# A graph layer on one core: one of four transposed chunks made by a block-wise load and VectorE, the sums turned elsewhere

## The chip, the core and the metric

The kernel runs on one core of a Trainium2 chip. The metric is the device time of one execution in microseconds. The kernel before took 223.35 us (median of 3 runs, 223.28 to 223.63).

## The reference

For each of 16 graphs there is a node matrix `x` (512 x 128) and an adjacency matrix `adj` (512 x 512), both float32. The layer normalises `x`, applies relu, and takes the maximum over seven relations.

```python
h = maximum(layernorm(x), 0)
A = [adj, adj, shifted, adj.T, adj.T, shifted.T, eye]          # by relation r = 0..6
HW = einsum('bnf,rfo->rbno', h, W[:, :F]) + einsum('rd,rdo->ro', W_edges, W[:, F:])[:, None, None, :]
AHW = einsum('rbnm,rbmo->rbno', A, HW)
out = x + AHW.max(axis=0) + b
```

As the reference calls it, both adjacency arguments are `adj`. `shifted` is the identity rolled by one row. The constant of each relation is multiplied by the row sums of `adj` (relations 0 and 1) or its column sums (3 and 4).

## The kernel before, in words

A batch is one graph. The order of the work is written out by hand for each engine, with semaphores between engines; there is no scheduler. Buffers that end in 0 and 1 are used by even and odd batches. Step `b` finishes the products of batch `b`, the relations of batch `b-1`, and prepares batch `b+1` ("ahead"). Steps 0 and 1 are unrolled, steps 2 to 13 are a loop of two steps, steps 14 and 15 are unrolled, and a tail follows.

Every float32 operand of a matrix product is split into a rounded part `_hi` and a remainder `_lo`, and each product is three matmuls (`passes`, lines 764 to 767: hi x hi, lo x hi, hi x lo). In one step TensorE does:

- `fwd` of chunks 0 to 3 (bank `fwd_ps`, from the transposed adjacency `at_hi`, `at_lo`) and `bwd` of chunks 0 to 3 (bank `bwd_ps`, from `a_hi`, `a_lo`), 24 matmuls;
- `eye` for three relations and `along` for four (of the batch before), 21 matmuls into the banks `rel_ps`;
- `turn_a` (line 734): for each column chunk `i` of `adj`, four 128x128 transposes against the identity into bank `at_ps[i % 2]`, for the batch ahead; chunks 0 and 1 after `along` of relation 1, chunks 2 and 3 at the end of the step;
- `turn_h` (four transposes of the activations) and `turn_sums` (one, of the 8 columns of sums, into `rel_ps[1]`; line 756).

ScalarE rounds each `adj` chunk to `a_hi` (`round_a`, line 384) and each transposed chunk to `at_hi` (`round_at`, line 389), and sums the rows as it does so; it also normalises, fills a relation's bank with sum times constant (`fill`, line 431), copies the turned sums to SBUF (`take_sums`, line 426) and writes the first relation to `best` (`join_first`). VectorE makes the remainders `at_lo` (`split_at`, line 562), `fwd_lo`, `bwd_lo` and `ht_lo`, takes the maxima (`join`) and turns the result (`turn_best`, which exchanges within 32x32 blocks). So that this is enough, the result is stored, and `x` and `bias` are loaded, by `load_by_blocks` and `store_by_blocks` (lines 201 to 208): four DMAs of 512 pieces of 128 bytes, which put each 32x32 block where its exchange needs it. GpSimd makes `a_lo` and `h_lo`, the inverse deviation, and the last additions.

SyncE starts the DMAs, in order: in a step it reloads `x` and the four chunks of `adj` for batch `b+2` (each waits for `a_lo` of its chunk), stores batch `b-2`, writes the sums to memory and reads them back broadcast over all partitions (`spread_sums`), and loads the blocks of `x`.

## Time and profile before

| | us |
|---|---|
| median of 3 runs | 223.35 |
| the profiled execution's own time | 223.7 |
| its span in the profile | 221.7 |
| TensorE busy | 211.5 (95%) |
| ScalarE busy | 186.0 (84%) |
| VectorE busy | 179.2 (81%) |
| GpSimd busy | 163.8 (74%) |
| DMA, share of 16 engines (the main queue) | 70.3% |

PE is TensorE, PEld its weight loads, DVE is VectorE, ACT ScalarE, POOL GpSimd, SPq the queue of SyncE. An engine's busy time counts overlapping instructions once. Matmuls are pipelined, so the time one costs is the distance from its start to the next start, and not its own length. The name of a line in the profile (L745) is a line of the kernel before; line numbers of the changed kernel are higher (`passes` is at lines 813 to 815, `turn_a` at 792, `turn_sums` at 810).

### The profile page before, as it was taken

How to read it: one execution, taken by the hardware profiler on the slowest of the kernel's cores; microseconds unless marked ns; L12 is line 12 of the kernel's file. 1: busy time of each engine (PE TensorE's matmuls, PEld its weight loads, DVE VectorE, ACT ScalarE, POOL GpSimd, SP SyncE). 2: the span in 40 equal slices, each digit the busy share in tenths (PEclk: the TensorE clock that was granted, in tenths of full speed). 3: DMA queues.
4: the chain of work that ended last, by engine and by line, in shares of the span. 5: the costliest groups of instructions: out<-in, count | busy, mean ns of one | idle time of the engine just before them, and what ended most of it. 6: DMA issues, size and time to landing. Idle time of an engine off the chain costs nothing.

```text
span 221.7 us, 4960 instructions
## 1 busy us (share of the span) xinstructions
PE 211.5 (95%) x1069; PEld 174.5 (79%) x1069; DVE 179.2 (81%) x388; ACT 186.0 (84%) x468; POOL 163.8 (74%) x179
## 2 busy tenths in 40 slices
PE   7898999999999999999999999999999999999980
PEld 5777678887888888888888888888888888887760
DVE  3795799796989879797887969887887969777683
ACT  3767999998998989898898989899898989887640
POOL 1370499979596996969697896969699696969241
PEclk9999999999999999999999999999999999999997
DMA  5928976959596986768596877758597776236725
GB/s 178 302 91 184 243 199 171 263 113 252 135 248 143 245 180 157 231 158 215 122 254 145 198 206 155 235 136 218 131 230 190 165 222 146 43 53 143 158 37 89
DMA packets 91152, 38.71 MB, mean 175 GB/s; under 512 B 71575, under 2 KB 80903, under 8 KB 91143
## 3 DMA queue, kind: packets, MB, share of 16 engines
q1 hardware_dynamic: 90055, 38.48, 70.3%
q10 hardware_dynamic: 1088, 0.13, 0.4%
q8 instruction: 3, 0.05, 0.1%
q14 instruction: 6, 0.05, 0.1%
HBM read 34.33 MB, written 4.26 MB: 174 GB/s over the span
## 4 chain that ended last, share of the span: by engine, by line
PE 85%; DVE 6%; ACT 2%; DMA 2%; issue 2%; SPq 0%; DVEq 0%; ACTq 0%
PE at_ps L745 11%; PE rel_ps L765 11%; PE rel_ps L767 11%; PE rel_ps L766 11%; PE bwd_ps L765 6%; PE bwd_ps L767 6%; PE bwd_ps L766 6%; PE fwd_ps L765 6%; PE fwd_ps L767 6%; PE fwd_ps L766 6%; PE turn_ps L753 3%; DMA a_sb<-in_adj 2%; DVE h_lo L692 1%; DVE best L595 1%; PE rel_ps L762 1%
## 5 line engine op out<-in xcount | busy, mean ns | idle before, releaser
L304 POOL TENSOR_TENSOR a_lo<-a_sb,a_hi 128x512 fp32r<-128x512 f32 x62 | 79.1, 1298 | 37.8 <-ACT a_hi L386 37.8
L595 DVE TENSOR_TENSOR best<-rel_ps,best 128x512 f32<-128x512 f32 x62 | 42.6, 687 | 13.7 <-PE rel_ps L767 13.6
L566 DVE TENSOR_TENSOR at_lo<-at_ps,at_hi 128x512 fp32r<-128x512 f32 x62 | 41.2, 685 | 8.2 <-ACT at_hi L394 7.6
L434 ACT ACTIVATE rel_ps<-sum_all,c_col 128x512 f32<-128x512 f32 (+1 forms) x63 | 41.8, 679 | 4.5 <-DVE best L595 2.9
L386 ACT ACTIVATE a_hi<-a_sb 128x512 fp32r<-128x512 f32 x64 | 39.4, 617 | 3.8 <-DMA a_sb<-in_adj 3.8
L394 ACT ACTIVATE at_hi<-at_ps 128x512 fp32r<-128x512 f32 x62 | 36.3, 590 | 6.5 <-PE at_ps L745 6.3
L745 PEld LDWEIGHTS at_ps<-ident,a_sb 128*128 128x128 f32 x240 | 28.1, 141 | 4.2
L745 PE MATMUL at_ps<-ident,a_sb 128*128 128x128 f32 x240 | 31.2, 272 | 0.0
L592 DVE SCALAR_TENSOR_TENSOR best<-rel_ps,c_col,best 128x512 f32<-128x512 f32 x32 | 23.9, 747 | 6.9 <-PE rel_ps L767 5.8
L319 POOL TENSOR_TENSOR xb_sb<-xp_sb,bias_sb 128x512 f32<-128x512 f32 x16 | 22.7, 1421 | 5.9 <-DMA xp_sb<-in_x 5.9
L765 PE MATMUL bwd_ps<-a_hi,h_hi 128*128 128x512 f32 x64 | 27.0, 421 | 0.0
L765 PE MATMUL fwd_ps<-at_hi,h_hi 128*128 128x512 f32 x64 | 26.6, 416 | 0.4 <-DVE at_lo L566 0.4
L767 PE MATMUL bwd_ps<-a_hi,h_lo 128*128 128x512 f32 x64 | 25.4, 397 | 0.0
L766 PE MATMUL bwd_ps<-a_lo,h_hi 128*128 128x512 f32 x64 | 25.3, 395 | 0.0
L767 PE MATMUL fwd_ps<-at_hi,h_lo 128*128 128x512 f32 x64 | 25.2, 394 | 0.0
L766 PE MATMUL fwd_ps<-at_lo,h_hi 128*128 128x512 f32 x64 | 25.1, 392 | 0.0
L404 ACT ACTIVATE h_sb<-x_sb,shift,rstd 128x128 f32<-128x128 f32 x60 | 24.6, 482 | 0.0
L765 PE MATMUL rel_ps<-ht_hi,w_hi 128*128 128x512 f32 x48 | 19.3, 403 | 1.4 <-issue 0.9
L326 POOL TENSOR_TENSOR o_sb<-turned,xb_sb 128x512 f32<-128x512 f32 x15 | 19.4, 1293 | 0.0
L767 PE MATMUL rel_ps<-ht_hi,w_lo 128*128 128x512 f32 x48 | 19.0, 396 | 0.0
L766 PE MATMUL rel_ps<-ht_lo,w_hi 128*128 128x512 f32 x48 | 19.0, 396 | 0.0
L312 POOL TENSOR_TENSOR h_lo<-h_sb,h_hi 128x512 fp32r<-128x512 f32 x14 | 18.1, 1294 | 0.4 <-DVE h_hi L560 0.4
(103 smaller groups left out, 438.9 us busy)
## 6 DMA issues: line engine op xcount, KB each, us to landing
a_sb<-in_adj SPq DMA_DIRECT2D x64, 256.0 KB, 3.3
sum_all<-sums_dram SPq DMA_DIRECT2D x16, 512.0 KB, 4.1
x_sb<-in_x SPq DMA_DIRECT2D x16, 256.0 KB, 3.7
xp_sb<-in_x SPq DMA_DIRECT2D x64, 64.0 KB, 3.6
out<-o_sb SPq DMA_DIRECT2D x60, 64.0 KB, 2.0
w_sb<-in_L_gnn_W SPq DMA_DIRECT2D x1, 448.0 KB, 6.0
sums_dram<-sum_rows SPq DMA_DIRECT2D x16, 4.0 KB
bias_sb<-in_L_gnn_b SPq DMA_DIRECT2D x4, 64.0 KB, 2.2
```

The costliest lines, as they stand in the source:

```text
L304: pool.tensor_tensor(a_lo[q][:, j, :], a_sb[q][:, j, :], a_hi[q][:, j, :].bitcast(fp32), ALU.subtract).then_inc(a_lo_ready[j], 1)
L386: act.activation(a_hi[q][:, j, :], a_sb[q][:, j, :], ACT.Copy, accum_out=sums[q][:, 0, j:j + 1]).then_inc(a_hi_ready[j], 1)
L394: act.activation(at_hi[q][:, i, :], at_bank(b, i)[:], ACT.Copy, accum_out=sums[q][:, 1, i:i + 1]).then_inc(at_hi_ready[i], 1)
L404: last = act.activation(h_sb[q][:, j, :], x_sb[q][:, j, :], ACT.Relu, bias=shift[q][:, j:j + 1], scale=rstd[q][:, j:j + 1])
L434: act.activation(to[:, cols], sum_all[q][:, 0 if r in FWD else 1, cols], ACT.Copy, scale=c_col[:, r:r + 1]).then_inc(after_it, 1)
L566: dve.tensor_tensor(at_lo[q][:, i, :], at_bank(b, i)[:], at_hi[q][:, i, :].bitcast(fp32), ALU.subtract).then_inc(at_lo_ready[i], 1)
L592: dve.scalar_tensor_tensor(out=best[q][:], in0=held[:], scalar=c_col[:, r:r + 1], in1=best[q][:], op0=ALU.add, op1=ALU.max).then_inc(joine ...
L595: dve.tensor_tensor(best[q][:], held[:], best[q][:], ALU.max).then_inc(joined[r], 1)
L745: last = pe.transpose(at_bank(b, i)[:, j * P:(j + 1) * P], a_sb[q][:, j, i * P:(i + 1) * P], ident[:])
L765: pe.matmul(out, w_hi_, m_hi, start=start, stop=False, skip_group_check=onto)
L766: pe.matmul(out, w_hi_, m_lo, start=False, stop=False, skip_group_check=onto)
L767: return pe.matmul(out, w_lo_, m_hi, start=False, stop=stop, skip_group_check=onto)
```

## The change

The last column chunk of `adj` is no longer transposed by TensorE (except for batch 0). SyncE loads `adj[b, :, 384:512]` once more by blocks, with the same four DMAs of 512 pieces of 128 bytes, into `a_blocks`; VectorE turns `a_blocks` into `at_last` in SBUF; `round_at` and `split_at` of chunk 3 read `at_last` in place of a PSUM bank. `a_blocks` and `at_last` are single buffers.

The sums are turned into `at_ps[0]` after `fwd` of chunk 1 (batches 2 to 15; for batch 15 that place is the one of before), and ScalarE takes them behind `join_first`. SyncE's step is reordered: `x` first, then the store of the sums, `adj` (as two DMAs of two chunks each), the broadcast, the output, the blocks of `x`, the new blocks. The first step is reordered on TensorE, ScalarE and VectorE.

In the diff "..." marks lines left out.

```diff
@@ -70,6 +71,8 @@
 a_lo = pair(sb, "a_lo", [P, C, N], fp32r)
+a_blocks = sb("a_blocks", [P, N])
+at_last = sb("at_last", [P, N])
 at_hi = pair(sb, "at_hi", [P, C, N], fp32r)
@@ -107,7 +110,14 @@
-def at_bank(b, i):
+def is_batch(b, n):
+
+    return isinstance(b, int) and b == n
+
+def at_from(b, i):
+
+    if i == C - 1 and not is_batch(b, 0):
+        return at_last
@@ -222,19 +230,30 @@
         b = 2 * k + q
-        sp.wait_ge(a_turned[C - 1], b + 1)
-        for j in range(C):
-            sp.wait_ge(a_lo_ready[j], b + 1)
-            load_a(k + 1, q, j)
+        sp.wait_ge(a_turned[C - 2], b + 1)
+        if is_batch(b, 0):
+            sp.wait_ge(first_turned, 1)
+        for first in range(0, C, 2):
+            sp.wait_ge(a_lo_ready[first], b + 1)
+            sp.wait_ge(a_lo_ready[first + 1], b + 1)
+            sp.dma_start(a_sb[q][:, first:first + 2, :],
+                         adj[2 * k + 2 + q, first * P:(first + 2) * P, :].rearrange("(j p) m -> p j m", p=P)
+                         ).then_inc(a_loaded[q][first + 1], 16)
+
+    def load_a_blocks(k, q):
+
+        b = 2 * k + q
+        wait(sp, a_turned[C - 1], b - 1)
+        load_by_blocks(a_blocks, adj[b, :, (C - 1) * P:], a_blocks_loaded)
+
+    def store_sums(k, q):
+
+        sp.wait_ge(sum_rows_ready, 2 * k + q + 1)
+        sp.dma_start(sums_dram[q][:, :], sum_rows[q][:]).then_inc(sums_stored[q], 16)
...
-        b = 2 * k + q
-
-        sp.wait_ge(sum_rows_ready, b + 1)
-        sp.dma_start(sums_dram[q][:, :], sum_rows[q][:]).then_inc(sums_stored[q], 16)
-        if is_batch(b, 0):
-            load_by_blocks(bias_sb, bias, bias_loaded)
+
@@ -246,17 +265,24 @@
-        sums_first = is_batch(2 * k + q, 0) or is_batch(2 * k + q, B - 1)
-        if sums_first:
-            spread_sums(k, q)
-        if more:
+        if more and not is_batch(2 * k + q, 0):
+            reload_x(k, q)
+        if is_batch(2 * k + q, 1):
+            reload_a(k, q)
+        store_sums(k, q)
+        if is_batch(2 * k + q, 0):
+            load_by_blocks(bias_sb, bias, bias_loaded)
+        elif more and not is_batch(2 * k + q, 1):
+            reload_a(k, q)
+        spread_sums(k, q)
+        if is_batch(2 * k + q, 0):
             reload_x(k, q)
...
             store(k - 1, q)
-        if not sums_first:
-            spread_sums(k, q)
         load_xp(k, q)
+        if more:
+            load_a_blocks(k + 1, q)
@@ -267,6 +293,7 @@
         load_a(0, 1, j)
+    load_a_blocks(0, 1)
     sp.dma_start(we_sb[:], W[:, F:FE, :]).then_inc(we_loaded, 16)
@@ -380,7 +407,8 @@
         b = 2 * k + q
-        act.wait_ge(a_loaded[q][j], 16 * (k + 1))
+
+        act.wait_ge(a_loaded[q][j if isinstance(k, int) and k == 0 else j // 2 * 2 + 1], 16 * (k + 1))
         wait(act, bwd_done, b - 1)
@@ -388,10 +416,13 @@
         b = 2 * k + q
-        act.wait_ge(a_turned[i], b + 1)
+        if is_batch(b, 0) and i == C - 1:
+            act.wait_ge(first_turned, 1)
+        else:
+            act.wait_ge(a_turned[i], b if i == C - 1 else b + 1)
         wait(act, fwd_done, b - 1)
         wait(act, sums_turned, b - 1)
-        act.activation(at_hi[q][:, i, :], at_bank(b, i)[:], ACT.Copy,
+        act.activation(at_hi[q][:, i, :], at_from(b, i)[:], ACT.Copy,
                        accum_out=sums[q][:, 1, i:i + 1]).then_inc(at_hi_ready[i], 1)
@@ -446,16 +477,16 @@
         act.activation(w_hi[:], w_sb[:], ACT.Copy).then_inc(w_hi_ready, 1)
-        take_sums(0, 0)
+        take_sums(0, 0, rel_ps[1])
         round_at(*ahead, 0)
...
         normalise(*ahead)
+        round_fwd(0, 0)
         act.wait_ge(c_ready, 1)
         join_first(0, 0)
-        round_fwd(0, 0)
-        round_ht(*ahead)
         round_at(*ahead, 2)
         round_at(*ahead, 3)
+        round_ht(*ahead)
         round_a(*ahead, 0)
@@ -466,9 +497,9 @@
             round_at(k, q, 3)
-        if not left:
-            take_sums(k, q, at_ps[0])
         join_first(k, q)
+        if not second:
+            take_sums(k, q)
         if second:
@@ -488,7 +519,8 @@
             round_at(*ahead, 0)
-            take_sums(k, q)
+            if second:
+                take_sums(k, q, rel_ps[1])
         else:
@@ -552,6 +584,14 @@
+    def turn_a_blocks(k, q):
+
+        b = 2 * k + q
+        dve.wait_ge(a_blocks_loaded, G * 16 * b)
+        if not is_batch(b, 1):
+            dve.wait_ge(at_lo_ready[C - 1], b)
+        dve.transpose(at_last[:], a_blocks[:]).then_inc(a_turned[C - 1], 1)
+
@@ -610,18 +650,19 @@
                           ALU.mult).then_inc(wedge_cols_ready, 1)
+        turn_a_blocks(*ahead)
         split_at(*ahead, 0)
...
         dve.wait_ge(c_multiplied, 1)
-        dve.tensor_copy(c_col[:], rel_ps[0][:, 0:R]).then_inc(c_ready, 1)
+        dve.tensor_copy(c_col[:], turn_ps[:, 0:R]).then_inc(c_ready, 1)
         round_h(*ahead)
+        split_fwd(0, 0)
         dve.wait_ge(h_hi_ready, 2)
...
                           ALU.subtract).then_inc(h_lo_ready, 1)
-        split_fwd(0, 0)
-        split_ht(*ahead)
         split_at(*ahead, 2)
         join(0, 0, EYE[1])
+        split_ht(*ahead)
         join(0, 0, EYE[2])
@@ -640,6 +681,7 @@
             round_h(*ahead)
+            turn_a_blocks(*ahead)
         join(*prev, FWD[1])
@@ -734,15 +776,20 @@
         if i == 0:
-            for j in range(C):
+            for j in range(C) if isinstance(k, int) and k == 0 else (1, 3):
                 pe.wait_ge(a_loaded[q][j], 16 * (k + 1))
-        if i >= 2:
-            pe.wait_ge(at_lo_ready[i - 2], b + 1)
+        if i == 2:
+            pe.wait_ge(at_lo_ready[0], b + 1)
+        elif i == 0:
+            pe.wait_ge(at_lo_ready[2], b)
+            if not is_batch(b, 2):
+                pe.wait_ge(sum_rows_ready, b)
         else:
-            pe.wait_ge(at_lo_ready[i + 2], b)
+
+            pe.wait_ge(at_lo_ready[C - 1 if is_batch(b, 1) else 1], b)
         for j in range(C):
-            last = pe.transpose(at_bank(b, i)[:, j * P:(j + 1) * P], a_sb[q][:, j, i * P:(i + 1) * P], ident[:])
+            last = pe.transpose(at_from(b, i)[:, j * P:(j + 1) * P], a_sb[q][:, j, i * P:(i + 1) * P], ident[:])
         last.then_inc(a_turned[i], 1)
@@ -753,12 +800,13 @@
-    def turn_sums(k, q, to=rel_ps[SUMS_BANK]):
+    def turn_sums(k, q, to=at_ps[0]):
         b = 2 * k + q
...
         pe.wait_ge(at_hi_ready[C - 1], b + 1)
-        if is_batch(b, 0):
-            pe.wait_ge(at_lo_ready[1], 1)
+
+        if not is_batch(b, 1):
+            pe.wait_ge(at_lo_ready[1 if is_batch(b, 0) else 2], b + 1)
         pe.transpose(to[0:S, 0:P], sums[q][:].rearrange("p t c -> p (t c)"), ident[:]).then_inc(sums_turned, 1)
@@ -809,8 +857,10 @@
         else:
-            pe.wait_ge(sum_rows_ready, b + 1)
-            if not (isinstance(b, int) and b == 0):
+
+            if is_batch(b, 0) or is_batch(b, 1):
+                pe.wait_ge(sum_rows_ready, b + 1)
+            if not is_batch(b, 0):
                 pe.wait_ge(joined[EYE[1]], b + 1)
@@ -838,24 +888,24 @@
         bwd(0, 0, 3)
-        turn_sums(0, 0)
+        turn_sums(0, 0, rel_ps[1])
         turn_a(*ahead, 0)
+        turn_a(*ahead, 1)
         fwd(0, 0, 1)
         fwd(0, 0, 2)
-        turn_a(*ahead, 1)
-        fwd(0, 0, 3)
         pe.wait_ge(we_loaded, 16)
         pe.wait_ge(wedge_cols_ready, 1)
-        pe.matmul(rel_ps[0][:, 0:R], we_sb[:], wedge_cols[:], start=True, stop=True).then_inc(c_multiplied, 1)
+        pe.wait_ge(ht_lo_ready, 1)
+        pe.matmul(turn_ps[:, 0:R], we_sb[:], wedge_cols[:], start=True, stop=True).then_inc(c_multiplied, 1)
+        fwd(0, 0, 3)
         pe.wait_ge(w_hi_ready, 1)
         pe.wait_ge(w_lo_ready, 2)
+        eye(0, 0, EYE[0])
+        turn_a(*ahead, 2)
         pe.wait_ge(c_ready, 1)
-        eye(0, 0, EYE[0])
+        turn_h(*ahead)
         eye(0, 0, EYE[1])
-        turn_h(*ahead)
         eye(0, 0, EYE[2])
-        turn_a(*ahead, 2)
-        turn_a(*ahead, 3)
@@ -863,9 +913,8 @@
         fwd(k, q, 1)
-        if not left:
-            pe.wait_ge(at_lo_ready[2], B)
-            turn_sums(k, q, at_ps[0])
+        if not is_batch(b, 1):
+            turn_sums(k, q)
         eye(k, q, EYE[1])
@@ -875,8 +924,9 @@
             turn_h(*ahead)
+        if is_batch(b, 1):
             pe.wait_ge(joined[EYE[1]], b + 1)
-            turn_sums(k, q)
+            turn_sums(k, q, rel_ps[1])
         bwd(k, q, 0)
@@ -886,7 +936,6 @@
             turn_a(*ahead, 2)
-            turn_a(*ahead, 3)
```

TensorE, end of a step and beginning of the next (steps of the loop). `bwd_ps` is the last `bwd`, `fwd_ps` the first `fwd` of the next batch. Before:

```order
L767 MATMUL bwd_ps<-a_hi,h_lo 128x512
L745 MATMUL at_ps<-ident,a_sb 128x128 x8
L765 MATMUL fwd_ps<-at_hi,h_hi 128x512
L766 MATMUL fwd_ps<-at_lo,h_hi 128x512
L767 MATMUL fwd_ps<-at_hi,h_lo 128x512
```

In the change, as far as the turn of the sums:

```order
L815 MATMUL bwd_ps<-a_hi,h_lo 128x512
L792 MATMUL at_ps<-ident,a_sb 128x128 x4
...
L813 MATMUL fwd_ps<-at_hi,h_hi 128x512
L814 MATMUL fwd_ps<-at_lo,h_hi 128x512
L815 MATMUL fwd_ps<-at_hi,h_lo 128x512
L810 MATMUL at_ps<-ident,sums 8x128
L813 MATMUL rel_ps<-ht_hi,w_hi 128x512
```

Four of the eight transposes at the step's end are gone, and the turn of the sums stands between the `fwd` of chunk 1 and the `eye` of relation 5.

VectorE, the middle and the end of a step in the change (`a_blocks` and `at_last` are the new buffers, `best` the running maximum):

```order
L600 CAST h_hi<-h_sb 128x512
L590 REGISTER_ALU
L593 STREAM_TRANSPOSE at_last<-a_blocks 128x512
L635 TENSOR_TENSOR best<-rel_ps,best 128x512
...
L642 STREAM_TRANSPOSE turned<-best 128x512
L606 TENSOR_TENSOR at_lo<-at_ps,at_hi 128x512
L606 TENSOR_TENSOR at_lo<-at_last,at_hi 128x512
L623 TENSOR_TENSOR bwd_lo<-bwd_ps,bwd_hi 128x512
```

The first transpose is new, and the remainder of the last chunk has both of its inputs in SBUF; before, the two remainders were one row, `at_lo<-at_ps,at_hi 128x512 x2`.

ScalarE, around the first relation. Before, and then in the change:

```order
L394 ACTIVATE at_hi,sums<-at_ps 128x512 [waits sums_turned,fwd_done,a_turned3]
L442 ACTIVATE best<-rel_ps,c_col 128x512 [waits best_turned,rel_done2]
L434 ACTIVATE rel_ps<-sum_all,c_col 128x512 [waits sums_spread0,joined3]
```

```order
L425 ACTIVATE at_hi,sums<-at_last 128x512 [waits sums_turned,fwd_done,a_turned3]
L473 ACTIVATE best<-rel_ps,c_col 128x512 [waits best_turned,rel_done2]
L460 ACTIVATE sum_rows<-at_ps 8x128 [waits sums_stored1,sums_turned]
L465 ACTIVATE rel_ps<-sum_all,c_col 128x512 [waits sums_spread0,joined3]
```

The copy of the sums has come between the first relation and the first fill.

## Rows read from the trace of the kernel before

**Rows 1.** The page: busy time of the engines, and the chain that ended last.
```profile
PE 211.5 (95%) x1069; PEld 174.5 (79%) x1069; DVE 179.2 (81%) x388; ACT 186.0 (84%) x468; POOL 163.8 (74%) x179
...
PE 85%; DVE 6%; ACT 2%; DMA 2%; issue 2%; SPq 0%; DVEq 0%; ACTq 0%
```

**Rows 2.** Windows: length, busy of PE, PEld, DVE, ACT, POOL, clock, DMA, GB/s.
```profile
12.00:24.00 12.00, 10.74 (x59) 8.64 (x58) 8.99 (x20) 8.69 (x23) 3.12 (x7) 1.00 0.61 152
48.92:112.44 63.52, 63.52 (x332) 53.00 (x331) 54.05 (x116) 57.16 (x146) 52.28 (x56) 1.00 0.77 194
```

**Rows 3.** Timeline of TensorE, one step: start, length, instruction.
```profile
118.08 1.03 PE L745 MATMUL at_ps<-ident,a_sb 128*128 128x128 f32 x8
118.95 0.60 PE L753 MATMUL turn_ps<-ident,h_sb 128*128 128x128 f32 x4
119.39 0.27 PE L762 MATMUL rel_ps<-ident,sums 128*8 128x128 f32 x1
119.41 0.48 PE L765 MATMUL bwd_ps<-a_hi,h_hi 128*128 128x512 f32 x1
119.73 0.40 PE L766 MATMUL bwd_ps<-a_lo,h_hi 128*128 128x512 f32 x1
119.96 0.39 PE L767 MATMUL bwd_ps<-a_hi,h_lo 128*128 128x512 f32 x1
```

**Rows 4.** Timeline of TensorE, the last step, around its turn of the sums.
```profile
203.31 0.40 PE L767 MATMUL fwd_ps<-at_hi,h_lo 128*128 128x512 f32 x1
203.54 0.27 PE L762 MATMUL at_ps<-ident,sums 128*8 128x128 f32 x1
...
203.88 0.39 PE L766 MATMUL rel_ps<-ht_lo,w_hi 128*128 128x512 f32 x1
...
204.81 0.40 PE L767 MATMUL fwd_ps<-at_hi,h_lo 128*128 128x512 f32 x1
205.31 0.50 PE L765 MATMUL rel_ps<-fwd_hi,w_hi 128*128 128x512 f32 x1
```

**Rows 5.** Timelines of TensorE, ScalarE and VectorE in one step.
```profile
112.44 0.48 PE L765 MATMUL fwd_ps<-at_hi,h_hi 128*128 128x512 f32 x1
...
116.00 0.39 PE L765 MATMUL rel_ps<-fwd_hi,w_hi 128*128 128x512 f32 x1
...
114.11 0.69 ACT L442 ACTIVATE best<-rel_ps,c_col 128x512 f32<-128x512 f32 x1 [0.43 <-PE rel_ps L767]
114.69 1.30 ACT L434 ACTIVATE rel_ps<-sum_all,c_col 128x512 f32<-128x512 f32 x2
...
113.22 1.29 DVE L566 TENSOR_TENSOR at_lo<-at_ps,at_hi 128x512 fp32r<-128x512 f32 x2 [0.22 <-ACT at_hi L394]
```

**Rows 6.** Groups by line: the transpose that VectorE already does.
```profile
L602 DVE STREAM_TRANSPOSE turned<-best 128x512 f32<-128x512 f32 x15 | 10.5, 703 | 0.0
```

**Rows 7.** Timelines of VectorE and GpSimd where both read SBUF.
```profile
9.30 0.29 DVE L692 TENSOR_TENSOR h_lo<-h_sb,h_hi 128x128 fp32r<-128x128 f32 x1
...
9.76 1.38 DVE L692 TENSOR_TENSOR h_lo<-h_sb,h_hi 128x128 fp32r<-128x128 f32 x1
...
9.71 2.57 POOL L304 TENSOR_TENSOR a_lo<-a_sb,a_hi 128x512 fp32r<-128x512 f32 x2 [3.44 <-ACT a_hi L386]
...
114.28 2.54 POOL L304 TENSOR_TENSOR a_lo<-a_sb,a_hi 128x512 fp32r<-128x512 f32 x2
```

**Rows 8.** Windows of the DMA share: one step; the start; only stores by blocks.
```profile
48.92:61.63 12.71, 12.71 (x68) 10.44 (x67) 10.71 (x23) 11.20 (x30) 9.98 (x12) 1.00 0.81 212
...
24.00:26.00 2.00, 1.50 (x7) 0.93 (x6) 1.86 (x10) 2.00 (x5) 1.25 (x1) 1.00 1.19 281
218.50:220.50 2.00, 0.00 (x0) 0.00 (x0) 0.00 (x0) 0.00 (x0) 0.00 (x0) 0.62 0.78 112
```

**Rows 9.** DMA issues and SyncE's queue: the loads of x by blocks.
```profile
xp_sb<-in_x SPq DMA_DIRECT2D x64, 64.0 KB, 3.6
...
109.69 1.92 SPq L203 DMA_DIRECT2D xp_sb<-in_x  x4
```

More of the change, by code:

```diff
@@ L35, in gnn_layer @@
     BANK = {EYE[0]: 0, EYE[1]: 1, FWD[0]: 2, FWD[1]: 0, BWD[0]: 2, BWD[1]: 0, EYE[2]: 1}
-    SUMS_BANK = 1
     S = 2 * C
@@ L162, in before @@
             return (k, 0) if q == 1 else (k - 1, 1)
-        def is_batch(b, n):
-            return isinstance(b, int) and b == n
         def rel_bank(b, r):
```

9 lines of the change are left out of this document (5 added, 4 removed).

## The prediction

> **What bounds the kernel now.** First the busy times and the chain of waits [rows 1]: TensorE is busy 95% of the span and holds 85% of the chain; no other engine holds more than 6%. Then the windows by stretch [rows 2]: over five steps in the middle, from 48.92 to 112.44, TensorE is busy all 63.52 us, so a step is 63.52 / 5 = 12.70 us of TensorE work and nothing else. VectorE is busy 54.05 / 5 = 10.81 us of it and idle 1.9, ScalarE 11.43 and idle 1.3. From 12 to 24 us, in the first step, TensorE is busy only 10.74 of 12.00 [rows 2]: there it waits. What TensorE no longer does in a middle step therefore comes off the time until the next engine is full, and the others have 1.3 to 1.9 us of room.
>
> **The terms.** The profiled execution took 223.7 us, 2.0 more than its span and 0.35 more than the median of the runs; I sum against 223.7 and take 0.35 off.
>
> 1. *Transposes of the last chunk.* Eight transposes stand at 118.08 and the next group starts at 118.95, four later ones take until 119.39 [rows 3]: 0.87 / 8 = 0.109 us each. The change removes four in each of batches 1 to 15, 60 in all: -6.5 us.
>
> 2. *The turn of the sums.* Among the other transposes it costs 0.03 us (119.39 to 119.41), and the first product behind transposes is followed after 0.32 us where later ones follow after 0.23 [rows 3]. In the last step it already stands alone between products: from the product at 203.31 to the second behind it, at 203.88, are 0.57 us, two distances of 0.23 and 0.11 more [rows 4]. The group behind which it stood keeps its own slow start. So each move costs 0.11 - 0.03 = 0.08 us, for batches 2 to 14, 13 times: +1.0 us.
>
> 3. *The last step.* There the relation at 205.31 starts 0.50 us after the product at 204.81, 0.27 more than the usual distance [rows 4]: it waits for a fill that stood behind the copy of the sums and the first relation. In the change ScalarE takes the first relation while TensorE is still in the `fwd` of chunk 1, so I count this wait as gone: -0.3 us.
>
> 4. *VectorE's new transpose.* The one it has on the same shape takes 0.70 us [rows 6], some 0.63 of it before the next instruction can start. Then 10.81 + 0.63 = 11.4 us stand in a step of 12.70 - 0.44 + 0.08 = 12.35: 0.9 idle instead of 1.9. Nothing, as long as no remainder comes late. The tight place is the new turn of the sums, which waits for `at_lo` of chunk 2. Before, the two remainders start at 113.22, so the first is done about 1.4 us after the step's first product at 112.44 [rows 5]; now chunk 2 is turned 0.44 later relative to that product, so it is done at about 1.8, and TensorE comes to the turn after three groups, at 3 x 0.70 = 2.1. The room is 0.3 us.
>
> 5. *ScalarE's copy of the sums ahead of the first fill.* The first relation starts 1.67 us into the step (114.11 against 112.44), the fill 2.25 in, and the relation that needs it starts at 116.00, 3.56 in [rows 5]. Now the copy waits for the turn: 2.1 + 0.27 for its result, so ScalarE starts it near 2.45 and the fill near 2.6, done near 3.3; the relation starts at 3.56 + 0.08. Room 0.3 us: no cost, but thin. In exchange, the fill of relation 4 no longer stands behind the copy.
>
> 6. *VectorE against GpSimd.* The remainder of chunk 3 now has two inputs in SBUF. A remainder of that kind takes 0.29 us at 9.30, and 1.38 us at 9.76, where GpSimd's own has started at 9.71 [rows 7]: it waited 1.1 us for it. In the middle steps GpSimd starts `a_lo` 1.84 us into the step (114.28), and VectorE comes to this remainder at about 1.6 to 2.0. So it may go first, and GpSimd, which has 11.3 us before its chunk 3 is needed, waits; or it waits up to 1.3 us. The trace has no such remainder in a middle step; its cost lies between 0 and, if every one waits in full and the 0.9 us of idle time do not cover it, 0.4 us a step, 5.6 us over 14 steps. Together with the thin room in 4 and 5 I take 0.3 us in two or three steps: +0.7 us, near the lower end, because most of VectorE's instructions can slip into idle time.
>
> 7. *DMA.* The new blocks are 2048 pieces of 128 bytes per batch. From 218.5 to 220.5 only such pieces move: share 0.78 at 112 GB/s [rows 8], so 256 KB of them are 2.3 us at that share, 1.8 us of all engines. A step has 0.77 x 12.7 = 9.8 us of DMA [rows 2], then 11.6 of 12.35, 0.94. Loads by blocks land after 3.6 us [rows 9]; SyncE issues the four in 1.9 us [rows 9], last in its step, and VectorE turns them in the middle of the next, some 6 us later: a backlog of 2 us is harmless. Two-chunk loads of `adj` carry the same bytes. Nothing on the path, bounds 0 and the rival below.
>
> 8. *The start.* The first step gets a load more in front of the small weights, and a VectorE transpose more; against that the wait for the constants ahead of the first `eye` goes, and that wait is part of the 1.26 us that TensorE lacks from 12 to 24 [rows 2]. Bounds -1.2 and +1.2 (the new transpose and half a microsecond of later landing); I take 0.
>
> Sum: 223.7 - 6.5 + 1.0 - 0.3 + 0.7 = 218.6, and 218.6 - 0.35 = **218.2 us**.
>
> The Trainium skill, page "SBUF — State Buffer", section "SBUF: two separate sides", says that VectorE with two SBUF inputs and a GpSimd instruction that reads SBUF exclude each other for a whole instruction, whoever starts first. The trace agrees: 1.38 us against 0.29 [rows 7]. By that rule alone every chunk-3 remainder that meets `a_lo` is blocked; that is rival A.
>
> **Rivals.**
>
> A. *VectorE becomes the bound through that exclusion.* For it: the two start within 0.3 us of each other, and the 1.38 us instruction. Against it: 0.9 us of idle time, and GpSimd yields when it comes second. Price: with half a blockage a step (0.6 us) and the cast's own waits already in the 10.81, VectorE has 12.0 us of work plus gaps it cannot close at the turns of `at_lo`; TensorE then loses about 0.2 us a step: 14 x 0.2 = 2.8 us on top, 218.2 + 2.8 = 221.0 us.
>
> B. *Slower: the DMA queue.* The mechanism: 2048 more small pieces in SyncE's one queue; `a_blocks` lands after VectorE reaches its transpose, and since VectorE works in order, every join and remainder behind it waits, and TensorE with them. The busiest step has a share of 0.81 [rows 8]. If the queue cannot hold more, a step takes 11.6 / 0.81 = 14.3 us, 1.6 more than now, for 12 steps: about 242 us. The point from which it decides is a sustained share of 11.6 / 12.70 = 0.91. Against it: from 24 to 26 us the share is 1.19 (several pieces in flight count together), and the present step leaves the queue idle because nobody asks.
>
> C. *No effect:* what TensorE saves in transposes it loses waiting for the turn of the sums, 0.36 us in each step (0.3 of room in 4 and 5 gone and as much again): 218.2 + 14 x 0.36 = 223.2 us. Only if VectorE were already late by 0.7 us at the end of each step; its idle time of 1.9 us speaks against it.
>
> The Trainium skill, page "DMA: Bandwidth & Descriptors", gives 512 bytes as the least transfer for full rate. The trace agrees in kind: 128-byte pieces move 112 GB/s while mixed traffic moves 281 [rows 8]. By it the loads are dear, but it does not say that they are late.
>
> **How the numbers follow.** Forecast 0.70, A 0.20, B 0.06, C 0.04. A measurement of this kernel can tell about 0.2% (0.45 us) from no change. Forecast and A are faster: 0.90; C is within 0.2%: 0.04; B is slower: 0.06. The forecast's own range takes term 8 and term 6: 216.4 to 219.8. The range for 8 in 10 has to reach most of A, so 216.5 to 221.2.
>
> **What would show it.** Right: in the middle windows TensorE is still busy throughout with steps of 12.3 to 12.4 us; 180 transposes under `turn_a`; VectorE near 11.4 us a step; the remainder from `at_last` mostly 0.7 us. Step 2 is wrong if the distance around the turn of the sums is not 0.57. A is right if the mean of the remainder from `at_last` is above 1.0 us and TensorE shows waits released by `at_lo` or a fill. B is right if VectorE's new transpose is released by the DMA of `a_blocks`. The start is right if `fwd` of batch 1 begins about 0.4 us earlier. What would make the prediction wrong is a wait in every step that these rows do not show, in the thin places 4 and 5.

## The result, and the profile after

The changed kernel took 224.75 us (median of 20 runs, 222.51 to 226.37); the kernel before, beside it on the same chip, 223.28 us (20 runs, 221.86 to 224.31). The ratio is 1.0044, 95% interval 1.0022 to 1.0065: slower, by about a microsecond, where 218.2 us with a range of 216.5 to 221.2 was forecast. The profiled execution took 224.81 us, with a span of 223.0.

The page of the kernel after: busy times, and the chain that ended last, by engine and by line.

```profile
PE 208.0 (93%) x1009; PEld 163.6 (73%) x1009; DVE 190.2 (85%) x403; ACT 183.4 (82%) x468; POOL 165.4 (74%) x179
...
SPq 34%; DMA 20%; issue 14%; ACT 12%; DVE 11%; PE 5%; POOL 2%; ACTq 1%; DVEq 0%; POOLq 0%
SPq L210 22%; DMA sums_dram<-sum_rows 10%; SPq L215 8%; DMA a_blocks<-in_adj 4%; DVE best L635 4%; ACT a_hi L414 3%; ACT h_sb L435 3%; DMA x_sb<-in_x 3%; DMA a_sb<-in_adj 2%; SPq L206 2%; ACT at_hi L425 2%; SPq L258 2%; DVE at_lo L606 2%; ACT rel_ps L465 1%; POOL a_lo L331 1%
```

Against [rows 1] the chain has changed hands. TensorE held 85% of it and holds 5%; SyncE's queue (line 210 issues the loads by blocks, line 215 the stores) and DMAs hold 54%. TensorE's busy share fell from 95% to 93%, although 60 transposes are gone and the span is longer: it waits now.

The same stretch of both kernels, 48.44 to 202.56, some twelve steps. The columns are those of [rows 2]. Before:

```profile
48.44:202.56 154.12, 154.12 (x803) 128.99 (x802) 129.71 (x271) 139.16 (x353) 127.52 (x134) 1.00 0.73 179
```

After:

```profile
48.44:202.56 154.12, 151.01 (x747) 119.79 (x746) 137.10 (x281) 134.75 (x348) 126.15 (x132) 1.00 0.84 199
```

TensorE was busy all of it; now it lacks 3.1 us. The DMA share of 0.84 does not look like a full resource. Nor does VectorE, with 137.10 of 154.12.

What the engines wait for in the kernel after (us in total, times, the longest):

```profile
ACT rel_ps L465 <- DVE best L635: 20.2, 17, 2.1
...
DVE at_last L593 <- DMA a_blocks<-in_adj: 4.3, 9, 1.1
PEld rel_ps L813 <- ACT rel_ps L465: 4.3, 8, 1.1
...
PE at_ps L810 <- DVE at_lo L606: 2.7, 10, 0.4
```

This is the sign that the prediction gave for rival B: VectorE's new transpose is released by the DMA of `a_blocks`. The wait travels: VectorE is late with the join behind it, ScalarE's fill waits for the join, TensorE's weight load for the fill. Only a part of the first row, ScalarE's wait for `best`, comes from there: it is 14.7 us also in `e1`, the run below in which no block is ever late (2.9 us before).

Where SyncE spends a step. Before, one step of its queue:

```profile
105.53 1.98 SPq L208 DMA_DIRECT2D out<-o_sb  x4
107.56 0.39 SPq L235 DMA_DIRECT2D sums_dram<-sum_rows  x1
109.16 0.35 SPq L239 DMA_DIRECT2D sum_all<-sums_dram  x1
...
112.26 0.70 SPq L199 DMA_DIRECT2D x_sb<-in_x  x1
113.20 4.11 SPq L212 DMA_DIRECT2D a_sb<-in_adj  x4
```

After:

```profile
105.61 0.39 SPq L206 DMA_DIRECT2D x_sb<-in_x  x1
106.05 0.40 SPq L252 DMA_DIRECT2D sums_dram<-sum_rows  x1
106.70 1.02 SPq L239 DMA_DIRECT2D a_sb<-in_adj  x2
108.61 0.35 SPq L258 DMA_DIRECT2D sum_all<-sums_dram  x1
109.21 2.32 SPq L215 DMA_DIRECT2D out<-o_sb  x4
111.72 4.07 SPq L210 DMA_DIRECT2D xp_sb<-in_x  x4
115.99 1.92 SPq L210 DMA_DIRECT2D a_blocks<-in_adj  x4
118.55 0.39 SPq L206 DMA_DIRECT2D x_sb<-in_x  x1
```

From one `x` to the next are 118.55 - 105.61 = 12.94 us, and the rows add up to 10.47 of it; 0.9 more, 107.72 to 108.61, is the wait until the stored sums are acknowledged, and the rest lies in gaps of 0.05 to 0.65 between issues, which stand before too. Nothing in it is a wait for an engine. Four issues by blocks took 1.92 us before [rows 9]; the four of `xp_sb` take 4.07 here. Three of them take the usual 0.35. The first takes 2.48, and around it the 16 DMA engines are busier than in the mean (the columns are those of [rows 2]):

```profile
111.72 2.48 SPq L210 DMA_DIRECT2D xp_sb<-in_x  x1
...
109.00:114.00 5.00, 4.74 (x22) 3.54 (x22) 5.00 (x16) 5.00 (x15) 2.37 (x3) 1.00 1.07 319
```

So the mean share of 0.84 hides a stretch at 1.07, and this one issue is held up in it. That the transfers ahead of it hold it up is the likely reading; no run tries it. SyncE's waits in the whole execution, before:

```profile
SPq L212 <- POOL a_lo L304: 27.1, 26, 1.8
SPq L208 <- POOL o_sb L326: 18.7, 14, 6.3
SPq L239 <- DMA sums_dram<-sum_rows: 17.9, 15, 2.3
SPq L235 <- ACT sum_rows L429: 7.2, 2, 5.3
```

After:

```profile
SPq L258 <- DMA sums_dram<-sum_rows: 14.2, 15, 2.8
SPq L215 <- POOL o_sb L353: 5.2, 2, 4.3
SPq L252 <- ACT sum_rows L460: 4.3, 2, 3.7
```

Before, SyncE waited 53 us for engines that were not ready; now 11 us (one more row, 1.5 us for `a_lo`, is left out), in few places at the ends. It runs round without slack in the steps between, and the kernel with it.

Three stretches of the two profiled executions beside the forecast (the last column is an experiment told of below). A start is that of the first `fwd` matmul of the batch.

| us | before | forecast | after | no loads (`e1`) |
|---|---|---|---|---|
| start to `fwd` of batch 2 | 35.99 | 35.1 | 35.55 | 35.01 |
| from there to `fwd` of batch 15 | 165.40 | 161.5 | 167.01 | 162.65 |
| from there to the end | 20.31 | 20.0 | 20.44 | 20.24 |
| span | 221.7 | 216.6 | 223.0 | 217.9 |

5.5 of the 6.4 us lie in the thirteen steps: 12.4 to 13.1 us each, 13.7 the last, where the terms gave 12.35 and a few waits.

### The profile page after: what moved, and what is told of

It is laid out like the page before. It is cut to its first block, busy times and chain, and to the rows that moved or that the text cites. A ratio compares the mean times of both kernels' runs of the same rounds, so it can differ in the third digit from the quotient of the medians.

```text
span 223.0 us, 4962 instructions
## 1 busy us (share of the span) xinstructions
PE 208.0 (93%) x1009; PEld 163.6 (73%) x1009; DVE 190.2 (85%) x403; ACT 183.4 (82%) x468; POOL 165.4 (74%) x179
## 4 chain that ended last, share of the span: by engine, by line
SPq 34%; DMA 20%; issue 14%; ACT 12%; DVE 11%; PE 5%; POOL 2%; ACTq 1%; DVEq 0%; POOLq 0%
SPq L210 22%; DMA sums_dram<-sum_rows 10%; SPq L215 8%; DMA a_blocks<-in_adj 4%; DVE best L635 4%; ACT a_hi L414 3%; ACT h_sb L435 3%; DMA x_sb<-in_x 3%; DMA a_sb<-in_adj 2%; SPq L206 2%; ACT at_hi L425 2%; SPq L258 2%; DVE at_lo L606 2%; ACT rel_ps L465 1%; POOL a_lo L331 1%
## 5 line engine op out<-in xcount | busy, mean ns | idle before, releaser
L635 DVE TENSOR_TENSOR best<-rel_ps,best 128x512 f32<-128x512 f32 x62 | 41.8, 675 | 10.2 <-PE rel_ps L815 10.1
L606 DVE TENSOR_TENSOR at_lo<-at_ps,at_hi 128x512 fp32r<-128x512 f32 x47 | 31.8, 681 | 0.8 <-ACT at_hi L425 0.5
L425 ACT ACTIVATE at_hi<-at_ps 128x512 fp32r<-128x512 f32 x47 | 27.8, 593 | 4.2 <-PE at_ps L792 4.2
L792 PE MATMUL at_ps<-ident,a_sb 128*128 128x128 f32 x180 | 24.6, 273 | 0.4 <-ACT sum_rows L460 0.4
L792 PEld LDWEIGHTS at_ps<-ident,a_sb 128*128 128x128 f32 x180 | 21.3, 141 | 4.9 <-issue 1.2
L813 PE MATMUL rel_ps<-ht_hi,w_hi 128*128 128x512 f32 x48 | 20.8, 434 | 0.5 <-issue 0.5
L600 DVE CAST h_hi<-h_sb 128x512 fp32r<-128x512 f32 x15 | 15.4, 1027 | 5.6 <-ACT h_sb L435 5.6
```

Source lines behind the costliest of these rows:

```text
L425: act.activation(at_hi[q][:, i, :], at_from(b, i)[:], ACT.Copy, accum_out=sums[q][:, 1, i:i + 1]).then_inc(at_hi_ready[i], 1)
L606: dve.tensor_tensor(at_lo[q][:, i, :], at_from(b, i)[:], at_hi[q][:, i, :].bitcast(fp32), ALU.subtract).then_inc(at_lo_ready[i], 1)
L635: dve.tensor_tensor(best[q][:], held[:], best[q][:], ALU.max).then_inc(joined[r], 1)
L792: last = pe.transpose(at_from(b, i)[:, j * P:(j + 1) * P], a_sb[q][:, j, i * P:(i + 1) * P], ident[:])
L813: pe.matmul(out, w_hi_, m_hi, start=start, stop=False, skip_group_check=onto)
```

## The experiments

Theory 1: SyncE's queue is full, and what it brings late (blocks, `x`, the sums) holds up VectorE and ScalarE. Theory 2: VectorE itself has too much in the places where TensorE waits for it. The runs are on three chips; each has the kernel before beside it (medians 223.3, 223.42 and 223.46).

### The loads taken away (`e1_no_block_loads`)

```diff
-                if more:
-                    load_a_blocks(k + 1, q)
...
-        dve.wait_ge(a_blocks_loaded, G * 16 * b)
+        dve.wait_ge(a_blocks_loaded, G * 16)
```

> The changed kernel without the loads of a_blocks for batches 2 to 15: VectorE turns the blocks of batch 1 again each time, so the last transposed chunk is wrong from batch 2 on; every compute instruction stays. Theory Q (SyncE's queue is full: its instructions and waits fill 12.8 us of a step, and the blocks land late): without the 1.9 us of four issues the queue has room, the waits of VectorE for a_blocks (4.3 us) vanish, a step is 12.35 to 12.45 us and the time 218.5 to 220. Theory V (VectorE, with one more transpose and its exclusion with GpSimd, is late for the turn of the sums and for the joins): nothing on VectorE is removed, a step stays 12.7 to 12.8 and the time 223.5 to 224.7.

Measured: 219.86 us (219.66 to 220.93), ratio 0.986, interval 0.9797 to 0.9923. The loads cost 4.9 us by the medians, 4.1 by the two ratios. Steps are 12.40 and 12.57 in turn, 12.48 in the mean, and SyncE waits for engines again (33.4 us for the rows of sums). TensorE lacks 0.67 us in twelve steps:

```profile
47.88:197.66 149.78, 149.11 (x748) 120.82 (x746) 136.66 (x282) 135.13 (x349) 126.53 (x133) 1.00 0.69 181
```

That busy time hides what is left over. Transposes saved, 0.44, and a turn of the sums that costs 0.02 (see `e8`) would make steps of 12.28. The timelines of this run, TensorE and then VectorE, in the step that begins at 110.24:

```profile
110.24 0.48 PE L811 MATMUL fwd_ps<-at_hi,h_hi 128*128 128x512 f32 x1
...
112.17 0.39 PE L813 MATMUL fwd_ps<-at_hi,h_lo 128*128 128x512 f32 x1
112.68 0.27 PE L808 MATMUL at_ps<-ident,sums 128*8 128x128 f32 x1
...
111.11 0.69 DVE L640 STREAM_TRANSPOSE turned<-best 128x512 f32<-128x512 f32 x1
111.85 0.69 DVE L604 TENSOR_TENSOR at_lo<-at_ps,at_hi 128x512 fp32r<-128x512 f32 x1
```

The turn of the sums could begin 0.23 behind 112.17. It begins 0.28 later, once `at_lo` of chunk 2 is there, which starts 1.61 into the step and ends 0.69 later. The distance that should be 0.57 [rows 4] (from the product ahead of the turn to the second one behind it) is 0.69 to 1.01 in batches 2 to 14, 0.79 in the mean. That is 0.22 a step, the whole way from 12.28 to 12.48. The window above shows only a quarter of it (0.67 us in twelve steps), since TensorE counts as busy while the matmul before the gap runs out.

### The loads kept, their data not used (`e2_loads_unused`)

```diff
-                    load_a_blocks(k + 1, q)
+                    b = 2 * k + q
+                    wait(sp, unused_loaded, G * 16 * b)
+                    load_by_blocks(unused, adj[b + 2, :, (C - 1) * P:], unused_loaded)
...
-        dve.wait_ge(a_blocks_loaded, G * 16 * b)
+        dve.wait_ge(a_blocks_loaded, G * 16)
```

> The changed kernel with all loads kept, but from batch 2 on into a buffer that nobody reads, so VectorE never waits for them (the last transposed chunk is wrong from batch 2 on). Theory Q, if it is the lateness of the blocks that counts: 219 to 221, near the run without loads. Theory Q, if the full queue delays whatever it carries (sums, x, adj): a step stays near 12.8 and the time at 223.5 to 225. Theory V: as the changed kernel, 224 to 225.

Measured: 222.4 us (10 runs, 220.65 to 223.44), ratio 0.9964 (0.993 to 0.9999). About half of the 4.9 us is the wait for the blocks themselves, and the other half stays when nobody waits for them. There `x`, the next in the queue, is late; VectorE's wait for it (2.6 us and 2 times in the kernel after; the profiled execution of `e2`, 220.9 us, was one of its fastest):

```profile
DVE stats L583 <- DMA x_sb<-in_x: 3.6, 7, 1.9
```

### The loads alone, in the kernel before (`e3_before_plus_loads`)

```diff
             load_xp(k, q)
+            if more:
+                b = 2 * k + q
+                wait(sp, unused_loaded, G * 16 * b)
+                load_by_blocks(unused, adj[b + 2, :, (C - 1) * P:], unused_loaded)
```

> The kernel before, with the four loads by blocks added at the end of SyncE's step, into a buffer that nobody reads; the result is the same. Theory Q: SyncE waits 60 us of the run before (3.7 a step), which takes up 1.9 us of issuing and some of the backlog; TensorE has 12.70 us of work anyway, so 223.3 to 225.5, with sums, x or adj awaited if it is above 224. Theory V: 223.0 to 223.6, the loads are free.

Measured: 242.58 us (4 runs, 238.35 to 244.76) against 223.3, 19 us more, for four loads a step that nobody reads. No theory expected it: the dearer of the two ranges ended at 225.5. That is rival B's price, 242 us, but not by B's sum: that took a share of 0.81 as the most that the queue holds, and this run's main queue has 73.0%. What is late is not a block. The waits of this run:

```profile
ACT rel_ps L440 <- DMA sum_all<-sums_dram: 23.6, 13, 2.3
PEld rel_ps L771 <- ACT rel_ps L440: 21.9, 14, 2.2
```

And SyncE's timeline at the end of its step:

```profile
115.99 1.46 SPq L237 DMA_DIRECT2D sums_dram<-sum_rows  x1
119.26 0.35 SPq L241 DMA_DIRECT2D sum_all<-sums_dram  x1
```

From the issue of the store of the sums to the issue of the broadcast are 3.27 us; before they were 1.60 (107.56 to 109.16, above). Of the 1.67 us more, 1.07 are the issue itself (1.46 against 0.39) and 0.6 the wait for its receipt. The 4 KB of sums stand behind the output's and all that came before, and SyncE stands still until they are acknowledged. The fills of the relations wait for the broadcast (13 times).

### The chunk in SyncE's old order (`e4_chunk_alone`, `e11_old_queue_order`)

`e4` keeps the chunk by VectorE, and undoes both moves of the sums (the turn at its old place on TensorE, the copy on ScalarE) and SyncE's order. `e11` undoes SyncE's order alone:

```diff
-                if more and not is_batch(2 * k + q, 0):
-                    reload_x(k, q)
-                if is_batch(2 * k + q, 1):
-                    reload_a(k, q)
-                store_sums(k, q)
...
-                elif more and not is_batch(2 * k + q, 1):
-                    reload_a(k, q)
-                spread_sums(k, q)
...
+                if more:
                     reload_x(k, q)
...
+                if not sums_first:
+                    store_sums(k, q)
+                    spread_sums(k, q)
                 load_xp(k, q)
```

> Of the change only the last chunk's way through a_blocks and VectorE (and the first step's order): the sums are turned and taken in the places of the kernel before, and SyncE's step has the order of before, with the blocks last. The result is the same as the reference's. Theory Q: the queue carries the same, and is full: 223.5 to 226, with a_blocks awaited. Theory V: the thin wait for at_lo of chunk 2 is gone, and so is the copy ahead of the first fill: 218.5 to 221.

> The changed kernel with one thing undone: SyncE's step in the order of the kernel before (x, adj, output, then the store of the sums and their broadcast, the blocks of x, the new blocks); the sums are still turned early; the result is the same. If the order of the queue is what saves the change from the 238 to 242 us of the runs with the old order: 234 to 242, with the fills waiting for the broadcast. If the early turn of the sums is what saves it: 224 to 227.

Measured: `e4` 238.24 us (237.62 to 238.67), ratio 1.0668 (1.0602 to 1.0735); `e11` 239.93 us (237.38 to 240.23), ratio 1.0706 (1.0641 to 1.0771). `e4` is beyond both of the ranges given for it; `e11` lies in the range for the order of the queue. The rows of `e11`: a wait of ScalarE and one of SyncE, and SyncE's timeline.

```profile
ACT rel_ps L464 <- DMA sum_all<-sums_dram: 17.9, 12, 2.0
...
SPq L258 <- DMA sums_dram<-sum_rows: 27.5, 15, 3.6
...
116.15 1.75 SPq L252 DMA_DIRECT2D sums_dram<-sum_rows  x1
119.70 0.35 SPq L258 DMA_DIRECT2D sum_all<-sums_dram  x1
```

The same picture as in `e3`. The broadcast itself is not slower than before (4.0 us to landing, 4.1 before): it is issued late. With the sums earlier in time (`e11`) or not (`e4`), what counts is where they stand in the queue. So the change's order of SyncE, which looks like an extra, is worth 15 us here: without it the chunk makes the kernel 7% slower.

### Two of the four output stores on ScalarE's queue (`e5_two_stores_act`)

```diff
-                    store(k - 1, q)
+                    if is_batch(2 * k + q, B - 1):
+                        store(k - 1, q)
+                    else:
+                        sp.wait_ge(out_ready, 2 * (k - 1) + q + 1)
+                        for g in range(G // 2):
+                            sp.dma_start(...)
...
+                if left and not (isinstance(k, int) and k == 0):
+                    act.wait_ge(out_ready, 2 * (k - 1) + q + 1)
+                    for g in range(G // 2, G):
+                        act.dma_start(...)
```

> The changed kernel, with two of the four stores of the output of batches 0 to 12 started by ScalarE's queue, where ScalarE waits for a join (1.2 us a step); the result is the same. Theory Q1 (SyncE's one queue is full: its issue times, back-pressure and receipt add up to 12.8 us): about 1.2 us of a step leave it, VectorE waits less for a_blocks, 221 to 222.8. Theory Q2 (the DMA engines are full, whichever queue feeds them): the same pieces move, 224 to 225.5.

Measured: 220.52 us (220.45 to 220.6), ratio 0.9875 (0.9815 to 0.9934): it beats both kernels. The loads are all there, the bytes are the same, the share of the DMA engines in the steps is higher than ever, and TensorE is where `e1` had it:

```profile
48.66:198.61 149.95, 149.08 (x747) 120.70 (x746) 136.60 (x282) 134.99 (x349) 126.37 (x133) 1.00 0.88 205
```

12.50 us a step over these twelve, beside 12.48 without any loads. So what was full was the one queue, and not the 16 engines behind it: they carry the same in a shorter step. SyncE has some room again, and waits for `a_lo` as it did before, though less (27.1 us there):

```profile
SPq L238 <- POOL a_lo L338: 5.8, 9, 1.3
...
106.97 5.46 SPq L210 DMA_DIRECT2D xp_sb<-in_x  x4
```

The second row shows that the gain is not in shorter issues: the four of `xp_sb` are held up for longer here than in the change, 5.46 us against 4.07, and the kernel is faster all the same. What left SyncE is the issuing of two stores. Whether it also helps that the DMA engines are fed from two queues at a time was not tried apart from that.

The Trainium skill, page "DMA: Bandwidth & Descriptors", section "Issuing engines are not separate DMA queues", says that issuing from several engines saves only the issuing engine's own time, which is usually small beside the transfer. The rows agree for one DMA: a store's issue takes SyncE 0.46 us in the mean of the changed kernel's middle steps, and it lands 4.7 us after. But one queue has 17 issues a step, so the small times add up, and moving two of them was worth 4 us. ScalarE's timeline shows why the two issues cost it nothing: they lie in the time for which it waits for a join (ACTq are its DMA issues; the first begins at 105.56).

```profile
106.09 0.44 ACTq L536 DMA_DIRECT2D out<-o_sb  x1
106.91 0.69 ACT L472 ACTIVATE rel_ps<-sum_all,c_col 128x512 f32<-128x512 f32 x1 [0.91 <-DVE best L648]
```

### The blocks earlier in the queue (`e7_blocks_early`, `e9_early_and_act`)

Two buffers `a_blocks`, and their loads first in SyncE's step instead of last; `e9` is that together with the edit of `e5`.

```diff
-        a_blocks = sb("a_blocks", [P, N])
+        a_blocks = pair(sb, "a_blocks", [P, N])
...
-                wait(sp, a_turned[C - 1], b - 1)
+                wait(sp, a_turned[C - 1], b - 2)
```

> The changed kernel with two a_blocks buffers instead of one, and the four loads first in SyncE's step instead of last, so that they are issued some 10 us earlier relative to their use; the result is the same. If only the lateness of the blocks costs: as the run with loads into an unread buffer, 221.5 to 223, and no wait of VectorE for a_blocks. If the full queue then delays the next in line (x or the sums): 223 to 225, with that wait in its place.

> Both: two a_blocks buffers with the loads first, and two of four stores on ScalarE's queue; the result is the same. Theory Q1: the queue has room and the blocks are early, so the step comes near the 12.49 us of the run without loads: 219.5 to 221.5. Theory Q2: 222 to 224.5.

Measured: `e7` 225.47 us (10 runs, 223.54 to 226.22), ratio 1.0076 (1.0037 to 1.0115), no better than the change. The wait for the blocks is gone, and another has come, again the next in line:

```profile
DVE stats L580 <- DMA x_sb<-in_x: 9.5, 12, 1.9
```

This order of what VectorE needs does not help the full queue. `e9`: 223.05 us (10 runs, 220.67 to 223.92), ratio 0.9988 (0.9949 to 1.0027), worse than `e5`. That is a miss for theory Q1, which said 219.5 to 221.5; it lies in the range of Q2. Its profiled execution was one of its fastest, 221.02 us, with steps like those of `e5` (12.51 us), so why the others are longer is not settled.

### Everything but the chunk (`e8_without_chunk`)

TensorE transposes all four chunks again, the loads and VectorE's transpose are gone; the new places of the sums, SyncE's order and the first step's order stay.

```diff
-            if i == C - 1 and not is_batch(b, 0):
-                return at_last
...
-                if more:
-                    load_a_blocks(k + 1, q)
...
-                turn_a_blocks(*ahead)
...
+                turn_a(*ahead, 3)
```

> The other parts of the change without the chunk: TensorE transposes all four chunks, no a_blocks and no VectorE transpose; the sums are turned in at_ps[0] behind the fwd of chunk 1, and SyncE's and the first step's order are those of the change; the result is the same. The forecast's term 2: 12.70 + 0.08 us of TensorE in a step, so 223.3 + 1.0 = 224.3 (223.7 to 224.9), unless the turn waits for at_lo as well (0.3 a step more, up to 228). Theory Q: SyncE's queue has room, no wait on DMA. If the order of the queue were a gain of its own, it would be below 223.3.

Measured: 222.62 us (221.35 to 223.5), ratio 0.9971 (0.9938 to 1.0004), not clearly different from before, and below the 223.7 to 224.9 that was expected. Its profiled execution was the fastest of its runs, 221.35 us, so its start may flatter it: `fwd` of batch 2 begins at 33.91, 2.1 us earlier than before. By the medians `e8` is 0.8 us faster than before in all; its last step is 0.4 us shorter and thirteen turns cost 0.3, so some 0.7 is left for the start. Steps are 12.73 us against 12.71. The turn of the sums costs 0.02, not 0.08, and the timeline shows where the rest comes back: without the turn behind them, the four transposes of `turn_h` take less.

```profile
104.39 0.60 PE L787 MATMUL turn_ps<-ident,h_sb 128*128 128x128 f32 x4
104.75 0.48 PE L800 MATMUL bwd_ps<-a_hi,h_hi 128*128 128x512 f32 x1
```

0.36 us from their start to the product, where it was 0.44 to the turn behind them [rows 3]. At its new place the turn takes the 0.57 that was forecast, in every step: the chunk alone brings the 0.69 to 1.01 of `e1`.

### Two variants of the best (`e10_chunk_from_batch2`, `e12_three_stores_act`)

`e10` is `e5`, with the last chunk of batch 1 left to TensorE too, so that the start has no load by blocks in front of its small weights. `e12` is `e10` with three of the four stores on ScalarE's queue:

```diff
-                        for g in range(G // 2):
+                        for g in range(1):
...
-                    for g in range(G // 2, G):
+                    for g in range(1, G):
```

> The version with two stores on ScalarE's queue, and in addition batch 1's last chunk is transposed by TensorE as batch 0's: no load of blocks in front of the small weights, no VectorE transpose in the first step; the result is the same. The kernel without the chunk reached the first fwd of batch 2 at 33.91 us, the version with two stores at 35.40. If the load at the start costs that: 1.0 to 1.5 us less than 220.5, so 219.0 to 219.6. If the start's loss comes from the loads of the first steps' end instead: 220.2 to 221.

> As the version that transposes batch 1 on TensorE, with three instead of two of the four stores on ScalarE's queue. If SyncE's queue still sets part of the step: 0.3 to 1 us faster. If ScalarE, which waits some 1.2 us a step at that place and needs 0.5 us per store, is now late: 0.5 to 3 us slower, with relation fills awaited by TensorE.

Measured: `e10` 220.51 us (6 runs, 220.23 to 223.84), ratio 0.9888 (0.9842 to 0.9935), the same as `e5` within its scatter: the 1.0 to 1.5 us that it was to give back at the start did not come. Its profiled execution is the slowest of the six, so its start cannot be read from it. `e12` 229.03 us (five of six runs 227.9 to 229.7; the sixth, at a granted clock of 0.56, took 343.8), ratio 1.0246 (1.0197 to 1.0295). ScalarE's timeline (its first issue is at 109.58):

```profile
110.20 1.15 ACTq L535 DMA_DIRECT2D out<-o_sb  x2
111.45 0.69 ACT L471 ACTIVATE rel_ps<-sum_all,c_col 128x512 f32<-128x512 f32 x1 [1.43 <-DVE best L646]
```

The third issue, some 0.6 us more, has no idle time to lie in: the fill begins 0.10 us behind it, not 0.38 as in `e5`, and TensorE's weight load waits for the fill 14 times, 7.0 us in all. The distance around the turn of the sums is 1.03 to 1.17 in steps 3 to 15. That the third issue is the cause follows from one edit against `e10`; that the whole 8.5 us go through this fill is read from the waits, not tried.

## Why the prediction was wrong

**The transposes (term 1)** were right. The 180 that are left stand under `turn_a`, and between `e8` and `e1`, which differ by the chunk, a step goes from 12.73 to 12.48: 12.73, less 0.44 for four transposes, and 0.22 more for what term 4 missed, is 12.51.

**The turn of the sums (term 2)** was over-sized: 0.02 us a step (`e8`) against 0.08. The 0.57 at its new place was right. At its old one the prediction took its cost as 0.03, and did not count that the transposes ahead of it end later, 0.44 against 0.36.

**The last step (term 3)** came in `e8`, where the end is 0.4 us shorter (19.91 us from `fwd` of batch 15, 20.31 before). In the changed kernel it is eaten up by the distance around the turn, 1.06 us instead of 0.57.

**VectorE's transpose (term 4)** is a step that failed, the lesser of two. It said that `at_lo` of chunk 2 is done about 1.8 us into the step, 0.3 before TensorE comes to the turn. In `e1` it is done at 2.3. Before, `turned`, which stands ahead of the remainders on VectorE, starts at 112.30, 0.14 ahead of the step's first product [rows 5]; in `e1` it starts 0.87 behind it, so 1.01 later. Traced back to the join behind `h_hi`: that join begins 6.87 us ahead of the next step's first product before (105.57), and 4.98 ahead in `e1` (105.26 against 110.24), 1.89 later. Those are 0.30 because this step of TensorE's is shorter (12.41 us against 12.71), 0.63 of the new transpose, 0.43 because `h_hi` takes 1.04 us instead of 0.61 (term 6), and 0.54 because `h_hi` starts later: ScalarE comes to normalising 4.02 us into its step, behind the copy of the sums, and not 3.48. From that join to `turned` VectorE took 6.73 us before and takes 5.85 in `e1`, with no wait left: 1.89 less 0.88 is the 1.01. The prediction had counted 0.44 alone and let the idle time of the whole step, 1.9 us, cover the rest; but most of it lies in the waits for joins and for `h_sb` nearer the step's beginning (0.64 us ahead of 115.08 in `e1`), where the new transpose cannot use it. Price: 0.22 us a step, 2.9 us over thirteen; in the changed kernel 0.34 a step, as all comes later there. This is theory 2, and it is true by that much.

**ScalarE's copy ahead of the first fill (term 5)** cost nothing, as said: in `e1` the first fill begins at 113.25 and the relation that needs it follows at the usual distance.

**The exclusion (term 6)** did not happen where it was looked for. The remainder from `at_last` takes 0.70 us in the mean of 15, where rival A needed more than 1.0. The two never meet: GpSimd's `a_lo`, too, comes later in the step now, 2.91 us into it in `e1` (1.84 before). It showed elsewhere, at the rounding of `h`. The group of `h_hi` in the kernel after (durations in ns: least, median, most):

```profile
L600 DVE CAST h_hi<-h_sb x15: 426/1056/1218, 18.3 to 194.9; 128x512 fp32r<-128x512 f32 x15
```

Before, its median was 768. It ends 0.28 to 0.29 us behind GpSimd's `o_sb`, whatever its own start: before 105.65 and 105.36, after 106.67 and 106.38, in `e1` 104.72 and 104.43, and so in all 13 steps of batches 2 to 14 after and in `e1`, and in 12 of 13 before. So it waits for the end of that addition, and only its start decides how long it seems. In `e8`, without the new transpose, the times go from 539 to 1515 ns with a median of 1019, and in 8 of 13 steps it ends 0.29 us behind the next GpSimd addition, `xb_sb`, instead. So the new order alone lengthens it already; how much of the 0.43 us in `e1` is the order's and how much the transpose's is open. The Trainium skill, page "SBUF — State Buffer", section "SBUF: two separate sides", counts a float32 copy from SBUF to SBUF among the instructions of VectorE that take the port shared with GpSimd, and the rows agree; the prediction had used the rule for two inputs only. Rival A's mechanism is here, at 0.43 us in the step followed above, and part of it reached TensorE by way of term 4.

**DMA (term 7)** is the step that decided. It said: 11.6 of 12.35 us of DMA, a backlog of 2 us, "harmless", nothing on the path. Its sizes were good (a share of 0.84 over the steps, against 0.94 by that sum), and its conclusion was wrong: it summed the 16 engines and never SyncE's own step, and it left the blocks 6 us of room on SyncE's place in the kernel before. In the changed kernel their last issue ends at 117.91, 5.2 us into the step that begins at 112.72, and VectorE turns them at 119.94. 2.0 us are left where 6 were counted, and a block lands 2.2 us after its issue (median). Three things in the runs stand behind it:

- The resource was not the 16 engines but SyncE's one queue. `e5` moves the same bytes at a share of 0.88 in 12.50 us a step.
- The time of an issue is not fixed. The 1.92 us for four issues come from the kernel before [rows 9]; in the changed one the four of `xp_sb` took 4.07, because one of them is held up for 2 us. That goes with the new order of the queue more than with the blocks, for the four take 4.22 in `e8`, which has none, with waits of SyncE for other engines still left, 34 us in twelve steps. The added load is the 1.92 us for the blocks' own four. Without the hold-up the round would be 10.8 us by this sum, but no run shows such a round.
- SyncE also holds a chain, store of the sums, receipt, broadcast, and all behind it waits for the receipt. A backlog ahead of it is dear: 19 us in `e3`, which is rival B's price. B had 0.06, for its price with an unlikely cause, late blocks. The cause that does cost as much is this chain, and the change had an answer to it in its own order of the queue, worth 15 us. What remained of B, 4 to 5 us, is in halves the late blocks and the late rest (`e1`, `e2`).

**The start (term 8)** was taken as 0 with bounds of 1.2. The new order of the first step gives 2.1 us in the profile of `e8`, its fastest execution, and some 0.7 by the medians; the chunk takes part or all of it back, 35.55 against 33.91 in the profiles. SyncE's timeline at the start, in the kernel after:

```profile
7.67 3.40 SPq L210 DMA_DIRECT2D a_blocks<-in_adj  x4
11.12 2.44 SPq L297 DMA_DIRECT2D we_sb<-in_L_gnn_W  x1
13.61 0.41 SPq L299 DMA_DIRECT2D wedge<-in_L_gnn_W_edges  x1
```

`wedge`, on which `c` hangs, is issued at 13.61, where `e8` issues it at 8.53 and the kernel before at 9.39. How much of the 1.6 us is that, and how much VectorE's transpose, is open: `e10`, which takes both away for batch 1, was no faster than `e5` beyond its scatter.

The sum, mended: 12.28 us a step and 0.22 for the late remainder make 12.50, which is `e1` and `e5`. The full queue adds 0.35 a step in the stretch from 48.44 to 202.56 of the kernel after (154.12 / 12 = 12.84), 4.5 us over thirteen steps, the 4 to 5 that `e1` and `e5` give back. That the queue was full is shown by these two runs; why the median of `e9`, with the same relief, is 2.5 us above `e5` stays open.

## What to carry to other kernels

Sum up the queue that issues the DMAs like an engine: every issue with the time for which it may be held up, plus every receipt it waits for, against the step; a mean DMA share well below 1 says nothing of it. A small store that is waited for and read back belongs ahead of the large transfers, and issues can go to a second engine's queue where that engine waits anyhow, as many as its wait holds (two here, not three). And when an engine is given work out of its idle time, look up where in the step the idle time lies: only what stands between the new work and the next thing others wait for covers it.
